# Expert weight bounds: ScalarE's running sum in place of VectorE's maximum, and the first matrix loaded ahead of the stack reads

## What is computed

```python
x = _layernorm(x + _L0_attn_ref(x, ...))
x = _layernorm(x + _L0_xattn_ref(ctx_1024, ctx_1024, x, mask, ...))
x = _layernorm(x + _L0_ffn_ref(x, ...))
# _L0_ffn_ref
probs = softmax(x_flat @ gate_w.T)
topk_probs, topk_idx = top_k(probs, 2)
hidden = relu(einsum('th,ehf->tef', x_flat, w1) + b1)
all_out = einsum('tef,efh->teh', hidden, w2) + b2
y_flat = sum(take_along_axis(all_out, topk_idx) * topk_probs)
```

## Time and profile before

| | us |
|---|---|
| median of 3 runs | 1413.37 (1411.68 to 1415.12) |
| the profiled execution, its own time | 1412.27 |
| its span, first to last instruction | 1410.2 |
| mean granted TensorE clock | 0.906 of full speed |
| VectorE busy in the span | 1022.0 |
| TensorE matmuls busy | 1091.7 |
| ScalarE busy | 567.4 |
| share of the DMA engines' time, SyncE's queue | 48.7% |

### The profile page before, as it was taken

The page is one execution under the profiler, slowest core; times in us unless marked ns, Lnnn a source line. Parts: engine busy times, 40 slices in busy tenths (PEclk is TensorE's granted clock), DMA queues, the critical chain, the costliest instruction groups (busy, mean ns, idle before and its releaser), DMA issues. The chain is left out here.

```text
span 1410.2 us, 32514 instructions
## 1 busy us (share of the span) xinstructions
PE 1091.7 (77%) x9874; PEld 772.1 (55%) x9875; DVE 1022.0 (72%) x2410; ACT 567.4 (40%) x1022; POOL 483.5 (34%) x597
## 2 busy tenths in 40 slices
PE   3778899889888888888885600088999999999980
PEld 2445666666655655565553400066777777777750
DVE  2579999999888989999985340066777777777764
ACT  1344555555545656665563200022323323332324
POOL 1233433433344343534322037612223223223324
PEclk7799999999999999999997555599999999999995
DMA  8489886678756887788754152275222222222227
GB/s 207 108 225 226 230 200 142 157 180 227 174 108 163 235 237 154 207 232 221 202 168 137 68 194 106 100 267 159 42 43 43 41 45 41 41 45 41 43 30 245
DMA packets 160383, 202.20 MB, mean 143 GB/s; under 512 B 30444, under 2 KB 141692, under 8 KB 157067
## 3 DMA queue, kind: packets, MB, share of 16 engines
q1 hardware_dynamic: 145864, 182.92, 48.7%
q0 software_dynamic: 13296, 17.83, 7.5%
q10 hardware_dynamic: 1152, 0.53, 0.2%
HBM read 122.63 MB, written 74.41 MB: 140 GB/s over the span
## 5 line engine op out<-in xcount | busy, mean ns | idle before, releaser
L1177 PE MATMUL HB<-xhi,W 128*128 128x128 f16 x2272 | 292.1, 221 | 21.7 <-issue 16.1
L1177 PEld LDWEIGHTS HB<-xhi,W 128*128 x2272 | 202.2, 98 | 65.8 <-issue 48.2
L1177 PE MATMUL HB<-xlo,W 128*128 128x128 f16 x1136 | 225.0, 220 | 0.0
L1460 POOL DMA_INDIRECT d_sums<-ysc,tok x71 | 111.0, 1563 | 327.3 <-DMA XB<-d_rows 171.7
L892 ACT ACTIVATE PT<-SB 128x1024 f32<-128x1024 f32 x128 | 131.1, 1024 | 138.3 <-PE SB L563 136.3
L659 DVE TENSOR_REDUCE mneg<-SA 128x4 f32<-128x1024 f32 x128 | 156.5, 1223 | 41.6 <-PE SA L515 39.5
L1177 PEld LDWEIGHTS HB<-xlo,W 128*128 x1136 | 111.9, 99 | 50.2 <-issue 0.7
L1370 DVE SCALAR_TENSOR_TENSOR hlo<-HB,hhi 128x512 f16<-128x512 f32 x142 | 98.2, 691 | 55.1 <-ACT hhi L1238 51.1
L1238 ACT ACTIVATE hhi<-HB 128x512 f16<-128x512 f32 x142 | 84.2, 593 | 121.3 <-DVE HB L1362 121.2
L1362 DVE SCALAR_TENSOR_TENSOR HB<-HB,SC,b1c 128x512 f32<-128x512 f32 x142 | 107.1, 754 | 16.7 <-PE HB L1177 11.9
L1246 ACT ACTIVATE ysc<-yb,wv 128x256 f32<-128x256 f32 x71 | 36.1, 508 | 191.8 <-DVE yb L1394 181.6
(11 more groups left out here) (195 smaller groups left out, 2500.4 us busy)
## 6 DMA issues: line engine op xcount, KB each, us to landing
wst<-in_w SPq DMA_DIRECT2D x32, 1024.0 KB, 10.0
d_w<-w SPq DMA_DIRECT2D x16, 1024.0 KB, 6.7
W<-d_w SPq DMA_DIRECT2D x8, 2048.0 KB, 8.7
k_stack<-d_k SPq DMA_DIRECT2D x96, 128.0 KB, 7.2
XB<-d_rows SPq DMA_DIRECT2D x71, 130.0 KB
d_rows<-fill SPq DMA_DIRECT2D x4, 1950.0 KB, 15.6
d_q<-q_part SPq DMA_DIRECT2D x16, 384.0 KB, 5.8
d_k<-k_part SPq DMA_DIRECT2D x16, 384.0 KB, 2.7
```

The costliest lines, as they stand in the source:

```text
L1177: mm = pe.matmul(out, w.rearrange("p e n -> p (e n)"), x[n % 2][:, k, :], start=(k == 0 and half == 0 and x is xhi), stop=(k == KT - 1 and ...
L1460: pool.indirect_dma_start(YS, bass.IndirectOffsetOnAxis(ap=tok[n % 6][:, 0:1], axis=0), ysc[n % 2][:, :], None, compute_op=ALU.add).then_i ...
```

## The change

VectorE's `weights` with its 64 reduces is taken out, and ScalarE gets `bounds`: at the end of each unit in mode "max" it runs an Abs activation over the quarter, whose sum along the row goes to the same place in `wmx`. The sum of absolute values is no less than the largest of them, so it is a bound too. The activation's elementwise output goes to `w16_0` or `w16_1`, which are otherwise unused in that mode. On SyncE, the write and the load of matrix 0 move, with their waits, ahead of the wait for the transposed scores and the reads of the q and k stacks.

```diff
--- before.py
+++ after.py
@@ -354,6 +354,14 @@
             if n == 0:
                 sp.dma_start(YS[T:T + P, :], fill[:, 0:D]).then_inc(sem("wr_fill"), 16)
 
+        def weights_of_first(i, mode):
+            experts_out(i - 1, mode, 0)
+            if mode == "scale":
+                wait(sp, "wmax0", NE)
+                experts_in(i, "halve", 0)
+            elif not (isinstance(i, int) and i in (7, B)):
+                experts_in(i, mode, 0)
+
         def step(i, mode):
             experts_in(i - 1, mode, 1)
             if on(i):
@@ -377,6 +385,9 @@
                              ).then_inc(sem("ld_cT"), 16)
             if on(i + 1):
                 write_parts("k", i + 1)
+            if not (isinstance(i, int) and i < 0):
+                weights_of_first(i, mode)
+            if on(i + 1):
                 wait_apart(sp, "ST", 2 * NG * (i + 1), "wr_mask", 16)
                 read_stack("q", i + 1, Q_RUNS)
                 read_stack("k", i + 1, k_runs)
@@ -386,13 +397,6 @@
                              ).then_inc(sem("ld_xT"), 16)
             if isinstance(i, int) and i < 0:
                 later_loads()
-            experts_out(i - 1, mode, 0)
-
-            if mode == "scale":
-                wait(sp, "wmax0", NE)
-                experts_in(i, "halve", 0)
-            elif not (isinstance(i, int) and i in (7, B)):
-                experts_in(i, mode, 0)
             if on(i):
                 write_parts("ck", i)
             if on(i - 2):
@@ -751,17 +755,6 @@
                 name, off = GAPS[u, half]
                 item(name, i + off, i)
 
-        def weights(u, i, mode):
-
-            if mode != "max":
-                return
-            k, c = divmod(u, NG)
-            wait(dve, f"ld_wst{k}", 16 * (i + 1))
-            ins = dve.tensor_reduce(wmx[:, k, c, bass.ds(i, 1)], wst[k][:, c * QW:(c + 1) * QW], AX.X, ALU.max,
-                                    apply_absolute_value=True)
-            if c == NG - 1:
-                ins.then_inc(sem(f"wmax{k}"), 1)
-
         def halves(u, i, mode):
 
             if mode != "halve":
@@ -812,7 +805,6 @@
                 top(u, 1, i)
                 split_maxima(u, i)
 
-                weights(u, i, mode)
                 if u:
                     halves(u - 1, i, mode)
                 gap(u, 1, i)
@@ -905,6 +897,18 @@
             wait(act, f"AV{c}", NG * b + g + 1)
             act.activation(avs[:, :], AV[:, 0:L], ACT.Copy).then_inc(sem(f"avs{c}"), 1)
 
+        def bounds(u, i, mode):
+
+            if mode != "max":
+                return
+            k, c = divmod(u, NG)
+            wait(act, f"ld_wst{k}", 16 * (i + 1))
+            scratch = w16[k][:, :, :].rearrange("p a n -> p (a n)").bitcast(F32)
+            ins = act.activation(scratch[:, c * QW:(c + 1) * QW], wst[k][:, c * QW:(c + 1) * QW], ACT.Abs,
+                                 accum_out=wmx[:, k, c, bass.ds(i, 1)])
+            if c == NG - 1:
+                ins.then_inc(sem(f"wmax{k}"), 1)
+
         def weights(u, i, mode):
 
             if mode != "halve":
@@ -930,6 +934,7 @@
                 exps(u, 1, i)
                 gap(u, 1, i)
                 first_part(u, 1, i)
+                bounds(u, i, mode)
                 weights(u, i, mode)
 
         iterations(step, act)
```

## The result

| | before | after |
|---|---|---|
| median of the runs, us | 1414.24 (4 runs, 1411.68 to 1419.43) | 1454.32 (4 runs, 1447.81 to 1455.78) |
| profiled execution, its own time | 1412.27 | 1455.78 |
| its span | 1410.2 | 1453.9 |
| mean granted TensorE clock | 0.906 | 0.893 |

The changed kernel takes 1.0267 times as long, interval 1.0243 to 1.0290: 40 us slower by the medians. The prediction was 1421 with a range up to 1432: the right side, by the right wait, but a fifth of the size and outside the range.

The account below looks back on a forecast made before the run. It took VectorE as the apparent bound, TensorE close behind, and SyncE's stack reads as closing the loop. 4 us gained and 12 lost made +8, 1420.3 against the profiled execution, 1421 us as median; range 1408 to 1432.

Parts of the forecast that it names:

- part 4: Halving iterations 9 to 14: write and load of 1 MB each ahead of the stack reads, 2.0 us lost each, 12 us.
- part 3: Maxima iterations: 1 MB load ahead of the stack reads delays them 0.6 to 0.7 us; 0.55 us an iteration, 4 us gained.
- The bound: Attention iterations: VectorE looks like the bound, TensorE 0.7 us behind, SyncE's stack reads closing the loop with under 1 us slack.
- VectorE was the bound after all: Rival, chance 0.15: removed reduces pull units forward, 3.0 us in each of 8 iterations, 24 us against 12 lost: 1401 us.
- Part 1: Maxima iterations: 64 reduces of 680 ns, 43.5 us, leave VectorE; 0.3 us gained before the stack reads, some 0.85 at most behind.
- Part 2: End of units in maxima iterations: 64 Abs passes added to ScalarE, 0.7 us each, bounds 0.63 and 1.35, costing nothing.
- The table loads: Rival, chance 0.03: Abs and Exp need different tables, two 1283 ns loads for each of 64 passes, about 1465 us.
- delay of the first scores: Halving iterations: first scores of the next batch late behind the moved transfers, 3.7 us in iteration 11, 1.7 in 13.
- taken off, since VectorE was late by itself: Halving iterations: the row maximum is later by only 2.6 us in iteration 11 and 0.6 in 13, mean 1.6.
- lost lead of TensorE: Halving iterations: TensorE loses its 1.76 us lead into the next batch; 0.4 us of it counted as lost.
- The clock: Rival, chance 0.11: TensorE idles some 3 us before six delayed batches, another 1.4 us each, 8 us: 1430 us.
- The cancelling case: Rival, chance 0.14: halving starts have more slack, 4 to 6 us lost against 4 gained, 1413 to 1416 us.

Follow-up runs that it names:

- e1: Changed kernel with SyncE's old order put back, so ScalarE's running sums alone; 1413.79 us, 0.9980 of the kernel before.
- e11: Old SyncE order, ScalarE's sums and VectorE's maxima both run in maxima iterations, the maxima into an unread tile; 1412.19 us, 0.9982 of the kernel before.
- e3: Changed kernel with the new SyncE order in the maxima iterations 0 to 7 alone; 1421.03 us, 1.0031 of the kernel before.
- e6: e1 with only the 1 MB load, and its wait, ahead of the stack reads in iterations 9 to 14; 1425.58 us, 1.0089 of the kernel before.
- e7: e1 with only the 1 MB write, and its wait, ahead of the stack reads in iterations 9 to 14; 1427.57 us, 1.0094 of the kernel before.
- e9: Changed kernel, new order in halving iterations only, plus 7 unread matmuls before the k stack wait in iterations 10 to 15; 1442.98 us, 1.0186 of the kernel before.
- e12: e1 with two unread matmuls ahead of the transposed scores in the fourth unit of every iteration; 1413.19 us, 0.9984 of the kernel before.

## Why the prediction was right in its direction and wrong in its size

The 1454 us lie outside the range because of two terms of the sum. The traces differ by 43.7 us where the sum had 8: of the 36 us between, 24 are part 4, whose 2.0 us an iteration are 6.05, and 13 part 3, whose 4 us gained are 8 to 9 lost.

**The bound: right.** VectorE's load decides nothing. The stack reads do in iterations 0 and 1 and in the halving iterations of the changed kernel; for the other maxima iterations it is argued above and not shown that TensorE's own order does. "VectorE was the bound after all" (0.15) is refuted by e1 and e11. What would have proved me wrong, maxima iterations under 41.5 us or first scores that don't wait for the k stack, did not come. But the k stack landed 17.6 to 19.6 us after the last transposed scores where I gave 16 to 18, and the halving iterations from 10 on took 51 to 53 us where I gave some 47.

**Part 1 and the gain of part 3: too high.** Of the reduces I counted 0.55 us an iteration as gained. Measured: 0 in iterations 3 to 7. The first row maximum comes earlier, but the next stretch is counted from the first scores, and these don't move.

**Part 2: right.** 0.826 us for 0.7, within 0.63 and 1.35; my upper bound had the second instruction that turned out to exist, at 199 ns and not 628. It is hidden: e11 has it on top of all that the kernel before does, and is no slower. The Trainium skill ("ScalarE: Activation LUTs", Rules for kernel authors) puts maxima on VectorE as the faster engine per element. Here ScalarE's main instruction is the faster one, 627 against 680 ns; with the reading of the sum the pass is the dearer one by 146 ns, as that rule has it, and this doesn't reach the span. The table loads (0.03) didn't come.

**Part 3, the load in front: wrong sign.** "4 us gained" was 8.8 us lost in iterations 0 to 7 by the two traces (some 2 of them by chance of the clock), 7.2 by the medians of e3 and e1. The failed step is "begins at 230.6, takes 2.6 us … delay 0.6 to 0.7": worked out for iteration 4 and then multiplied by eight. The rows of iteration 4 have a pause of the queue, those of iteration 1 none, and there the k stack was already what TensorE waited for. For iterations 3 to 5 the step holds: the load costs nothing there. The gain it was set against wasn't there either.

**Part 4: the mechanism right, the size a third.** This is the larger failed step. I took 2.0 us an iteration, 12 in all; measured 6.05, 36 in all. In its terms:

| us an iteration | predicted | measured |
|---|---|---|
| delay of the first scores (stretch b) | 2.7, the mean of 3.7 and 1.7 | 4.19 |
| taken off, since VectorE was late by itself | −1.1 | 0 |
| lost lead of TensorE | +0.4 | 0 |
| lower clock behind the wait (stretch a) | 0 | 1.86 |
| sum | 2.0 | 6.05 |

The delay: from the first packet of the write to the landing of the k stack I had 5.1 + 11.4 = 16.5 us; the windows of the changed kernel show 571.00 to 589.13, 18.1. The first two of these windows moved 331 and 349 GB/s, 2.1 MB in 6.1 us, which is the write and the load by themselves; in iteration 11 before they had 426 and 406 GB/s and took 5.1 us. So 1.0 us of the 1.6 are a slower write and load, and 0.6 the stacks, 12.03 for 11.4 us. Why they are slower isn't shown. The 5.1 us were a quick case, though: in the windows 604.20:610.00 and 695.30:701.70 of the kernel before, at its own write and load of iterations 12 and 14, the rate is 387 and 354 GB/s, so one iteration was too few to take a rate from. The deduction: I measured lateness at the first row maximum, where VectorE's own 1.76 us seemed to absorb a part. But a batch's path to its transposed scores starts at its first scores, so the whole delay is passed on; this was the step that the rows of before could have corrected, since both cuts were in them.

**The clock: named, and underpriced.** I gave it 0.11 and 1.4 us an iteration as a rival; it was the changed kernel's second term, 1.9 us. The 0.96 of iteration 13 had shown the fall without any wait for a DMA, so the wait of some 3 us that I expected should have had it in the forecast. With the measured terms in place of mine, the sum is 6 × 6.05 + 7 = 43 us above 1413, 1456 or 1457 against the measured 1454: no further term is needed.

The cancelling case (0.14) rested on "iterations like 13 are the rule", with a wait of 0.6 us; e6 and e7 show one megabyte alone already over the slack.

**Open.** Why the clock doesn't fall in one iteration and does in the next of the same kernel, as in iterations 0 to 2, where stretch a is 28.5 to 33.4 us among kernels with the same TensorE work; why the write and the load were slower ahead of the stacks; what holds the maxima iterations at 43.3 us; and whether the removed pass is worth the 0.2%.

## What to carry to other kernels

On this queue, which served its transfers in the order of issue, bulk transfers with half an iteration of time don't belong in front of the reads that the next batch waits for: behind the reads they cost nothing that the runs show, and ahead of them everything beyond the slack (here 1.0 us an iteration for the first megabyte, 3.1 for the second), and then the clock's. Check the pause that is to hide a transfer in every kind of iteration, the first ones too, and not in one. Cut an iteration where the loop is closed (here scores, transposed scores, stack reads) and count a delay there, not at an engine that happens to be late already.

## What the runs showed of the hardware

- An activation with a running sum is two instructions, 627 ns and an ACTIVATION_READ_ACCUMULATOR of 199 ns. Abs, with one table load in the whole trace, took no other table than its neighbours.
- After waits of 3.2 to 5.1 us for a DMA, TensorE's granted clock was at the lower level at the start of each of six batches, so that four score matmuls took 1.03 instead of 0.60 us; 3 us of unread matmuls in that wait kept it at 1.00 at all six starts in e9, and through the whole of its iterations 12 and 13. The clock also fell at single starts after waits of 1.6 and 1.9 us (e6, e7). With two such matmuls in a short pause of the fourth unit, e12's trace has no fall in iterations 9 to 14, where the traces with the old order and no fill have two or three.
- One megabyte written and one loaded took 6.1 us ahead of the stack reads (331 and 349 GB/s) and 5.1 us behind them in iteration 11 (426 and 406 GB/s); the reason isn't shown.
